# An attention and expert block: gate logits from the raw rows and centred weights, and two of four chunks routed inside the last attention round

## The reference, cut to what matters

```
x = x + attention(_layernorm(x))        # softmax(Q K^T / 4) V, then @ Wo + bo
h = _layernorm(x)
gate_logits = h @ gate_w.T              # 8 logits a row
top_vals, top_idx = top_k(gate_logits, 2)
w = softmax(top_vals)
x = x + sum over the two chosen e of w_e * (h @ expert_w[e].T + expert_b[e])
```

## Time and profile before

| | us |
|---|---|
| three runs | 1721.37, 1722.83, 1723.59 (median 1722.83) |
| profiled execution, its own time | 1721.14 |
| its span in the trace | 1719.2 |
| TensorE busy | 1634.2 (95%) |
| VectorE, ScalarE, POOL busy | 83%, 75%, 33% |
| share of the chain of waits that is TensorE | 87% |
| first product with Wo starts | 1447.31 |
| first slot's transposes start | 1537.85 |
| TensorE's last product ends | 1695.67 |
| mean granted clock of TensorE | 0.981 |

### The profile page before, as it was taken

The page is one execution under the profiler, slowest core; times in us unless marked ns, Lnnn a source line. Parts: engine busy times, 40 slices in busy tenths (PEclk is TensorE's granted clock), DMA queues, the critical chain, the costliest instruction groups (busy, mean ns, idle before and its releaser), DMA issues.

```text
span 1719.2 us, 38275 instructions
## 1 busy us (share of the span) xinstructions
PE 1634.2 (95%) x13793; PEld 797.7 (46%) x13794; DVE 1423.8 (83%) x1694; ACT 1286.5 (75%) x2417; POOL 564.4 (33%) x828
## 2 busy tenths in 40 slices
PE   6999999999999999999999999999999999876994
PEld 3533444444444444444444444444444445655883
DVE  4488999999999999999999999999999942645455
ACT  3226888888888888888888888888888897333552
POOL 3121243333333333333333333333333445333221
PEclk9999999999999999999999999999999999978997
DMA  6434345423343333233223323322322142754566
GB/s 202 114 104 118 74 100 113 85 67 91 76 90 71 91 76 76 67 91 86 69 67 91 73 81 84 98 67 67 91 68 35 42 138 71 290 190 134 154 210 252
DMA packets 86838, 179.03 MB, mean 104 GB/s; under 512 B 20206, under 2 KB 24318, under 8 KB 85936
## 3 DMA queue, kind: packets, MB, share of 16 engines
q1 hardware_dynamic: 50464, 87.22, 21.2%
q0 software_dynamic: 34656, 88.26, 16.4%
q10 hardware_dynamic: 1584, 1.57, 0.3%
HBM read 91.14 MB, written 86.23 MB: 103 GB/s over the span
## 4 chain that ended last, share of the span: by engine, by line
PE 87%; DMA 3%; POOL 2%; issue 2%; ACT 2%; DVE 1%; SPq 1%; another core or an unknown queue 1%; ACTq 0%; POOLq 0%; DVEq 0%
PE bank L1026 32%; PE bank L987 25%; PE bank L1016 14%; PE bank L1112 6%; PE bank L957 5%; PE bank L1158 1%; DMA x_all<-in_L_attn_x 1%; ACT o_acc L815 1%; PE bank L1204 1%; PE bank L978 1%; DMA scratch<-y_rows 1%; POOL x_all L531 1%; PE bank L1218 1%; DMA sums<-o_acc 0%
## 5 line engine op out<-in xcount | busy, mean ns | idle before, releaser
L1304 DVE TENSOR_REDUCE max_kc<-bank 128x1 f32<-128x1024 f32 x1024 | 1243.4, 1222 | 64.9 <-PE bank L987 48.9
L838 ACT ACTIVATE arena_p<-bank 128x512 f32<-128x512 f32 x2048 | 1109.7, 595 | 160.6 <-PE bank L1016 120.7
L1026 PE MATMUL bank<-arena_p,v_cur 128*32 128x256 f32 x8192 | 653.5, 391 | 10.6 <-ACT o_acc L815 10.6
L987 PE MATMUL bank<-k_st,q_st 48*128 48x512 f32 x2048 | 511.2, 496 | 0.8 <-ACT qf L785 0.8
L1016 PE MATMUL bank<-q_st,k_st 50*128 50x512 f32 x2048 | 441.6, 406 | 0.8 <-ACT arena_p L838 0.8
L987 PEld LDWEIGHTS bank<-k_st,q_st 48*128 48x128 f32 x2048 | 190.5, 183 | 428.3 <-issue 398.7
L1016 PEld LDWEIGHTS bank<-q_st,k_st 50*128 50x128 f32 x2048 | 295.1, 185 | 33.0 <-ACT arena_p L838 21.7
L1026 PEld LDWEIGHTS bank<-arena_p,v_cur 128*32 128x32 f32 x8192 | 162.4, 108 | 296.3 <-issue 152.3
L483 POOL DMA_DIRECT2D sums<-o_acc x128 | 64.8, 513 | 343.3 <-ACT o_acc L815 338.0
L957 PE MATMUL bank<-xT,arena_p 128*128 128x512 f32 x160 | 84.9, 644 | 5.7 <-DMA arena_p<-in_L_attn_bv 3.6
L486 POOL DMA_DIRECT2D sums_rec<-sums x32 | 18.2, 570 | 210.6 <-DVE sums L1334 210.6
(11 more groups left out here) (193 smaller groups left out, 1015.8 us busy)
## 6 DMA issues: line engine op xcount, KB each, us to landing
slots_x<-pad_row POOLq DMA_DIRECT2D x27, 1295.0 KB, 5.8
q_st<-q_parts SPq DMA_DIRECT2D x192, 128.0 KB, 4.4
xs<-slots_x SPq DMA_DIRECT2D x39, 259.0 KB
q_parts<-parts SPq DMA_DIRECT2D x16, 512.0 KB, 3.2
we_raw<-in_L_ffn_expert_w POOLq DMA_DIRECT2D x8, 1024.0 KB, 6.1
at_parts<-o_hl POOLq DMA_DIRECT2D x128, 64.0 KB, 2.3
we_his<-o_hl POOLq DMA_DIRECT2D x32, 256.0 KB, 2.4
we_hi<-we_his SPq DMA_DIRECT2D x8, 1024.0 KB
```

The source lines that it names most:

```text
L838: act.activation(probs[:, u % PRING, :], bank[:, ring_bank(("score", u)), :], ACT.Exp, scale=SCALE).then_inc(p_ready, 1)
L987: return pe.matmul(bank[:, 2 + 2 * (m % 2) + q, :], q_st[r:r + CROW, j % SLOTS, h, qt * P:(qt + 1) * P], k_st[r:r + CROW, key_slot(j // NC ...
L1026: mm = pe.matmul(bank[32 * h:32 * h + 32, 6, half], v_cur[:, kt, :], probs[:, (REP * kt + h) % PRING, half], start=(kt == 0 and part == 0) ...
L1304: dve.reduce_max(max_kc[:, m:m + 1], bank[:, 2 + 2 * (m % 2):4 + 2 * (m % 2), :].rearrange("p a s -> p (a s)"), AX.X).then_inc(m_done, 1)
```

## The change

**What it does.** With the second layer norm written out, a logit is (r·(W − mean W))·rstd, r being the raw row and mean W each expert's mean weight, so the row need not be normalised before the gates. The raw row is x + attention·Wo + bo. The x part comes from the first layer norm's rows, times their standard deviation: eight centred gate columns are put behind the 128 columns of Wv (`GV` = 136), with the mean taken off by `centre_gates`. The part of `bo` is four small products. Attention's part uses Wo·gates: Wo is transposed in round 30 (`turn_wo`), multiplied with the gates (`wo_gates`) and kept as `wowc`. A chunk's logits are then eight products of `wowc` with the chunk's attention outputs (`gate_logits`). Choices need no rstd; the difference of the two logits gets it inside the exponential.

Chunks 0 and 1 are routed in round 31 (table `GATES`: key tile, step), chunks 2 and 3 at tiles 8 and 12. Per tile, ScalarE keeps only the square root and TensorE only the three terms, in four banks. Scatters 0 to 3 are issued within and behind `divide_outputs(N)`, each tile's scatter waiting for its own statistics. `biases_split` moves from tile 9 to tile 6, `load_attention(1)` also waits for Wo·gates, `place_rows(3)` goes to slot 0, and the last additions for three chunks to slots 1, 2 and 3. At the start the loads get semaphores of their own, bv is no longer waited for before the projection, weights go over ScalarE's queue, and the loads of x's chunks 1 to 3 wait for Wk and Wq.

The diff, cut to its core:

```diff
-        GT_BANKS = [n % 2 for n in range(NKT - 2)] + [2, 3]
+        WO_BANKS, LG_BANK, RK_BANK, XT_BANK = (2, 3, 0, 1), 4, 5, 6
+        TURN_WO, WO_GATES = (11, 12), 14
+        LOGITS_AT, BACK_AT, RANKS_AT = {8: 2, 12: 3}, {8: 2, 12: 3}, {10: 2, 15: 3}
+        GATES = {3: ("logits", 0), 5: ("back", 0), 6: ("logits", 1), 8: ("ranks", 0), 10: ("back", 1), 13: ("ranks", 1)}
...
+            def scatter(n):
+                c = n // TT
+                if n == 0:
+                    pool.wait_ge(fill_dma, 16 * -(-NX // FILL))
+                    pool.wait_ge(tok_ready, NC - 1)
+                if n % TT == 0:
+                    pool.wait_ge(slots_ready, c + 1)
+                    if c == NC - 1:
+                        pool.wait_ge(tok_ready, NC)
+                pool.wait_ge(nmr_ready, n + 1)
+                for a in range(2):
+                    pool.indirect_dma_start(slots_x, bass.IndirectOffsetOnAxis(ap=slot_i[:, a, n:n + 1], axis=0),
+                                            x2_all[:, n, :], None).then_inc(sc_dma[c], 16)
...
                 pool.dma_start(sums_rec.rearrange("h (a q) -> (h a) q", a=32), sums[:, :]).then_inc(rec_dma, 16)
+                if i == N:
+                    scatter(0)
                 pool.wait_ge(rec_dma, 16 * i)
                 for h in range(REP):
                     pool.dma_start(rec_b[32 * h:32 * h + DK, :], sums_rec[h].partition_broadcast(DK)).then_inc(recb_dma, 16)
+                if i == N:
+                    scatter(1)
...
             divide_outputs(N)
+            for n in range(2, TT):
+                scatter(n)
             add_bias_o(NC - 1)
...
+            sp.wait_ge(wk_dma, 16)
+            sp.wait_ge(wq_dma, 16)
             for c in range(1, NC):
                 sp.dma_start(x_all[:, c * TT:(c + 1) * TT, :], x_t[:, c * TT:(c + 1) * TT, :]).then_inc(x_dma[c], 16)
+            for t in range(TT):
+                sp.dma_start(bv_sb[:, t, :], bv.partition_broadcast(P)).then_inc(bv_dma, 16)
...
                 if c == 1:
                     sp.wait_ge(v_ready, G)
+                    sp.wait_ge(ww_full, 1)
...
+            act.dma_start(wk_sb[:, :, :], Wk.rearrange("(k p) n -> p k n", p=P)).then_inc(wk_dma, 16)
+            act.wait_ge(consts, 6)
+            act.dma_start(wg_sb[:, :, 0:E], gate_w.rearrange("(k p) n -> p k n", p=P)).then_inc(wg_dma, 16)
+            act.dma_start(wq_sb[:, :, :], Wq.rearrange("(k p) n -> p k n", p=P)).then_inc(wq_dma, 16)
+            act.dma_start(bo_col[:, :], bo.rearrange("(k p) -> p k", p=P), allow_slow_non_contiguous=True).then_inc(bc_dma, 16)
+            act.dma_start(wv_sb[:, :, 0:KVD], Wv.rearrange("(k p) n -> p k n", p=P)).then_inc(wv_dma, 16)
...
-            act.wait_ge(fill_dma, 16 * -(-NX // FILL))
-            act.wait_ge(pv_done, PRING // REP + NKT * N)
-            for n in range(NKT + 2):
-                if n >= 3:
-                    gate_evac(n - 3)
-                if n >= 6 and n % TT == 2:
-                    logits_evac((n - 6) // TT)
-                if 1 <= n <= NKT:
-                    deviation2(n - 1)
-                    normalise_tile(n - 1)
+            for n in range(NKT):
+                deviation2(n)
+                if n in LOGITS_AT:
+                    logits_evac(LOGITS_AT[n])
...
+                    pe.wait_ge(wk_dma, 16)
+                if c == 0:
+                    pe.wait_ge(wg_dma, 16)
+                    pe.wait_ge(pool_step, 4)
+                    for k in range(KD):
+                        mm = pe.matmul(bank[:, 5, 304:304 + E], ones[:, :], wg_sb[:, k, 0:E], start=(k == 0),
+                                       stop=(k == KD - 1))
+                    mm.then_inc(gm_full, 1)
...
+            pe.wait_ge(gm_taken, 2)
+            pe.wait_ge(bc_dma, 16)
+            for k in range(KD):
+                mm = pe.matmul(bank[:, 5, 304:304 + E], bo_col[:, k:k + 1].to_broadcast([P, P]), wg_sb[:, k, 0:E],
+                               start=(k == 0), stop=(k == KD - 1))
+            mm.then_inc(bg_full, 1)
...
+            def turn_wo(j):
+                if j == 0:
+                    pe.wait_ge(wo_dma, 16)
+                    pe.wait_ge(m_done, 2 + MUNITS * N)
+                for k in range(KD):
+                    mm = pe.transpose(bank[:, 2 + j, k * P:(k + 1) * P], wo_raw[:, k, j * P:(j + 1) * P], ident[:, :])
+                mm.then_inc(woT_full, 1)
+            def wo_gates():
+                pe.wait_ge(woT_evac, KD)
+                for k in range(KD):
+                    for j in range(KD):
+                        mm = pe.matmul(bank[:, 2, k * 32:(k + 1) * 32], wo_t[:, j, k * P:(k + 1) * P], wg_sb[:, j, :],
+                                       start=(j == 0), stop=(j == KD - 1))
+                mm.then_inc(ww_full, 1)
+            def gate_logits(k):
+                if k == 0:
+                    pe.wait_ge(ww_ready, 1)
+                else:
+                    pe.wait_ge(lgT_ready, k)
+                pe.wait_ge(at_dma[k % 2], 32 * (k // 2 + 1))
+                for part in range(2):
+                    for d in range(KD):
+                        mm = pe.matmul(bank[32 * d:32 * d + 32, LG_BANK, :], wowc[:, d, :],
+                                       at_hl[k % 2][part][:, d, :].bitcast(F32), start=(part == 0), stop=(part == 1),
+                                       skip_group_check=True)
+                mm.then_inc(lg_full, 1)
...
+                if i == N - 2 and kt in TURN_WO:
+                    for j in range(2):
+                        turn_wo(2 * TURN_WO.index(kt) + j)
+                if i == N - 2 and kt == WO_GATES:
+                    wo_gates()
+                if i == N - 1 and kt in GATES:
+                    gates_step(*GATES[kt])
...
+            def attention_tile(n):
                 c, q = n // TT, slice(n % TT * P, (n % TT + 1) * P)
-                if term == 0:
-                    pe.wait_ge(at_dma[c % 2], 32 * (c // 2 + 1))
-                    pe.wait_ge(x2_ready, n + 1)
-                part, w = [(0, wo_hi), (1, wo_hi), (0, wo_lo)][term]
-                for k in range(KD):
-                    mm = pe.matmul(bank[:, WO_BANKS[n % 3], :], at_hl[c % 2][part][:, k, q], w[:, k, :],
-                                   start=(term == 0 and k == 0), stop=(term == 2 and k == KD - 1))
-                if term == 2:
-                    mm.then_inc(wo_full, 1)
...
-            pe.wait_ge(wc_dma, 16 * (2 + E))
+                pe.wait_ge(at_dma[c % 2], 32 * (c // 2 + 1))
+                if n >= len(WO_BANKS):
+                    pe.wait_ge(x2_ready, n - len(WO_BANKS) + 1)
+                product(bank[:, WO_BANKS[n % len(WO_BANKS)], :],
+                        [lambda k: at_hl[c % 2][0][:, k, q], lambda k: at_hl[c % 2][1][:, k, q]],
+                        [lambda k: wo_hi[:, k, :], lambda k: wo_lo[:, k, :]]).then_inc(wo_full, 1)
...
             for n in range(NKT):
-                attention_tile(n, 0)
-                if n >= 3:
-                    gate_logits(n - 3)
-                attention_tile(n, 1)
-                if n >= 6 and n % TT == 2:
-                    logits_back((n - 6) // TT)
-                attention_tile(n, 2)
-                if n >= 7 and n % TT == 3:
-                    ranks((n - 7) // TT)
-                if n >= 2:
-                    gate_transpose(n - 2)
-            gate_logits(NKT - 3)
-            gate_transpose(NKT - 2)
+                if n in LOGITS_AT:
+                    gate_logits(LOGITS_AT[n])
+                attention_tile(n)
+                if n in BACK_AT:
+                    logits_back(BACK_AT[n])
+                if n in RANKS_AT:
+                    ranks(RANKS_AT[n])
...
+            def centre_gates():
...
+                dve.wait_ge(gm_full, 1)
+                dve.wait_ge(wv_dma, 16)
+                sums_ = bank[:, 5, 304:304 + E].unsqueeze(1).to_broadcast([P, KD, E])
+                dve.scalar_tensor_tensor(wv_sb[:, :, KVD:GV], sums_, -1.0 / D, wg_sb[:, :, 0:E], ALU.mult,
+                                         ALU.add).then_inc(gm_taken, 1)
...
+            def evacuate_values(b):
+                tiles, both = slice(2 * b, 2 * b + 2), bank[:, 4 + b % 2, 0:2 * GV].rearrange("p (t n) -> p t n", t=2)
+                g0 = chosen[:, tiles, :]
+                dve.wait_ge(v_full, b + 1)
+                dve.tensor_tensor(v_all[:, tiles, :], both[:, :, 0:KVD], bv_sb[:, 0:2, :], ALU.add).then_inc(v_evac, 1)
+                dve.tensor_tensor(g0, both[:, :, KVD:GV], std2[:, tiles].unsqueeze(2).to_broadcast([P, 2, E]),
+                                  ALU.mult).then_inc(g0_evac, 1)
+                dve.wait_ge(g0_evac, b + 1)
+                dve.tensor_tensor(g0, g0, bo_gate[:, :].unsqueeze(1).to_broadcast([P, 2, E]), ALU.add).then_inc(g0_step, 1)
...
+            for j in range(KD):
+                turned_wo(j)
+            lower_wo()
+            take_gates()
+            logits_evac(0)
+            reciprocal_sums(N - 1)
+            choose_first(0)
```

(32 more changed lines are left out.)

352 lines of the change are left out of this document (159 added, 193 removed).

## The result

The changed kernel takes 1746.28 us (median of four runs, 1741.88 to 1749.87) against 1722.91 us for the kernel before (four runs, 1721.37 to 1723.59): the ratio is 1.0124, with a 95% interval of 1.0100 to 1.0148. The profiled execution took 1749.63 us, its span is 1747.9. Of the four executions two took 1741.88 and 1742.92 us at a mean granted clock of 0.973 and 0.974, and two 1749.63 and 1749.87 at 0.967 and 0.965: one slow stretch of 17 us fewer would make that difference of the clock (an estimate: 17 us at half clock are 0.005 of the span). The table is of the longer kind.

A forecast was written before the change was run, and what follows sets the result against it. TensorE was taken as the bound (95% busy, 87% of the chain of waits). Start -1.5, rounds +8, Wo stage +8 and slots -19 summed to -4.5 us on 1721.1, giving 1716.6 us, range 1700 to 1729.

The forecast's parts named there:

- The rounds: Rounds 30 and 31: 13.9 us of work inserted on TensorE, partly hidden, adds 8 us; bounds +4 and +13.9.
- each insertion is hidden for about 0.6 us: Rounds 30 and 31: ScalarE's queued score banks cover about 0.6 us of each of nine insertions, 5.4 us in all.
- the upper bound: Rounds 30 and 31: none of the inserted work is hidden, +13.9 us.
- rival 3: Rounds 30 and 31: insertions hidden as far as the queue allows, 1711 us, or (upper side, chance 0.10) not at all, 1722.5.
- The Wo stage: First Wo product to slots: DVE waits for memset and biases, delaying the serial chain; +8 us, bounds -12 and +20.
- rival 2: Wo stage: TensorE at the 1.2 GHz level through tiles 8 to 15, +11.5 us, total 1728 us; chance 0.16.
- the small load cannot pass the large ones: Wo stage: the bias load queues behind 9.44 MB of loads, landing about 46.3 us after the first Wo matmul.
- Rival 1: Wo stage: transfers don't hold DVE, so the chain ends 11 us earlier, total 1705.6 us; chance 0.24.
- The slots: The 39 slots: the gap before slot 9 goes, 138.6 us in all, -19 us; bounds -20 and -10.
- rival 4: Slots: slot 9 is still late by half of the gap, +9 us, total 1725.6 us; chance 0.08.
- The start: Kernel start: the projection no longer waits for bv, less added small matmuls, -1.5 us; bounds -3.0 and +3.
- the lower bound of -3.0: Kernel start: the most it could gain, the projection beginning at 14.82 us instead of 17.82.

The follow-up runs named there:

- e7_filler: e6 plus one unread 512-column product behind each turn-back and each ranks step in round 31; ratio 0.9984 to the kernel before.
- f2: Kernel before plus 1, 1 and 5 unread products of 512 columns at key tiles 11, 12 and 14 of round 30; ratio 1.0013.
- f3: Kernel before plus 16 unread 128-column transposes at key tiles 11 and 12 of round 30; ratio 0.9994.
- e1: Changed kernel with biases_split back behind tile 9; median 1736.92 us, ratio 1.0079 to the kernel before.
- e2: Changed kernel with the 16 products of Wo with the gates in four pieces at key tiles 13, 14, 15 and 0; ratio 1.0100 to the kernel before.
- e3: Changed kernel with attention chunk 2 issued before all weight loads, chunk 3 and the biases after two of them; median 1740.51 us, ratio 1.0109 to the kernel before.
- e6: e5 with the products of Wo with the gates in four pieces, as in e2; median 1713.93 us, ratio 0.9936 to the kernel before.
- after: The profiled execution of the changed kernel itself, with no further edit; 1749.63 us.
- e4: Changed kernel with scatters 2 and 3 behind the bias addition of chunk 3; median 1748.99 us, ratio 1.0147 to the kernel before.
- e5: Changed kernel with biases' memset, load and split later (split behind tile 15), ranks of chunk 2 behind tile 11, attention chunks issued as in e3; 1719.71 us, ratio 0.9970.
- r1: The changed kernel run again unaltered on another group's chip; median 1747.63 us, ratio 1.0144 to the kernel before.
- f1: Kernel before plus 16 unread 128-column transposes and 16 unread 32-column products in round 30; median 1747.99 us, ratio 1.0142.
- f5: Kernel before plus only the unread 32-column products at key tile 14 of round 30; ratio 1.0121.
- f4: f1 plus two unread 512-column products at key tile 15 of round 30 and two at key tile 1 of round 31; ratio 1.0039 to the kernel before.
- e8: e6 with the logits of chunk 1 behind the first ranks in round 31; ratio 0.9986 to the kernel before.
- r2: e6 run again beside r1 on one chip; median 1708.68 us, ratio 0.9924 to the kernel before.

## Why the prediction was wrong, step by step

**The rounds (+8 forecast, +27.8 measured) are the step that failed**, and twice. First, "each insertion is hidden for about 0.6 us" was wrong. Where the clock stayed up (e7_filler, less its 3.7 us of filler) the rounds took 69.5, 14.1 more than before: the whole of the 13.9 us of inserted work, which was the upper bound and the upper side of rival 3. f2 and f3 show the same in the kernel before, 6.5 us for 6.5 of work and 2.0 for 2.1. TensorE writes the scores just ahead of ScalarE, so ScalarE's wait (1.50 us behind 1.02 of transposes) was longer than the insertion. The trace of the kernel before had it already, in ScalarE's timeline of round 30, where ScalarE waits for scores between some key tiles, so that no scores lay in reserve:

```profile
1403.50 2.06 ACT L838 ACTIVATE arena_p<-bank 128x512 f32<-128x512 f32 x4 [0.18 <-PE bank L1016]
1405.74 2.06 ACT L838 ACTIVATE arena_p<-bank 128x512 f32<-128x512 f32 x4 [0.18 <-PE bank L1016]
```

Second, the sum had no term for the clock here. Traces with one slow stretch of 17 to 20 us have rounds of 75.3 to 77.7 (e1, e2, e3, e6), with two 81.9 to 84.8 (after, e4, e5, r1): 6 to 8 us for each. I read the falls of the clock in the earlier trace rows as the price of idling, and looked for them only where TensorE would wait. That reading was too simple for the kernel before, too, where not "each such wait" is followed by a slow stretch: the one of 2.19 us at 1471.73 is not. In round 30 the clock fell while TensorE was busy in every window. The experiments showed the trigger of that stretch (32-column products with the weight loads full, f1 and f5 against f2 and f3) and the cure (512-column products, f4). The trigger of the stretch in round 31 is not shown.

**The Wo stage (+8, +14.2)**: the mechanism was right, its size was off. Forecast and measured, in us after the first Wo product: VectorE idle until 31, then 29.5; the biases land at 46.3, then 49.1; the turn-back of logits 2 at about 54, then 55.2; tile 10 ends at 63.9, then 64.1; the ranks of chunk 2 at 68.7, then 70.3; the last product at 92, then 96.3; the slots at 98.5, then 104.8. So 1.0 of the 6.3 us too much had arisen by the turn-back and 4.3 by the last product; the last 2.0 lie behind it, where TensorE waits 4.23 us for VectorE before the ranks of chunk 3. What the 3.3 us in between are was not taken apart. Slow clock is the likely part of it, which would be rival 2 in part: its sign, 0.50 in most windows from 50 us on, held for 27 of 55 us, and between tile 7 and the slots the granted clock was at 0.50 for some 45 us (22 in the whole stage before), in part of which TensorE idled. That the small load cannot pass the large ones held: e3 moved it in the queue and it landed 9 us after the memset in place of nearly 20, e4 gave the memset 5 us and it landed no sooner. Rival 1, with transfers that do not hold VectorE, is thereby excluded (it is also the rival meant where the prediction says "the second rival's time"). Not foreseen was that attention chunk 2 itself came 9.09 us late for tile 8, behind two weight loads; VectorE's lag covered it.

**The slots (-19, -14.1)**: the gap before slot 9 is gone, as forecast, and rival 4 with it. The 39 slots cost 39 x 3.44 = 134.2, and 9.6 beside it where I had 4: the first takes 7.42, at slow clock, with a wait of 0.43 in it, and four more waits of 0.56 to 1.48 us on ScalarE and VectorE lie in the slots up to slot 8. No run was made to take these apart.

**The start (-1.5, -0.3)**: the sign was right; one trace of each says little. The first product for the maxima comes at 76.92, 80.42, 77.66, 79.35, 78.82 and 79.65 us in the six traces with the old start (mean 78.8), and at 73.2 to 76.8 in the twelve with the new one (mean 75.5); the gain is about 3 us, the lower bound of -3.0. The first projection began at 14.27, as forecast near 15.

**The sum**: in the traces, 14 us of work moved to where TensorE was full, 14 more of slow clock there, and 14 in the Wo stage, where VectorE waits for the memset and the biases, against 14 from the slots.

## What to carry to other kernels

Before work is put into a stretch where TensorE looks as if it had slack, see who sets the pace there and how far ahead TensorE is: with none, every microsecond counts in full. Here narrow products in pieces of 1.1 us, or with 512-column products behind them, cost little more than their own time in round 30; read the granted clock behind such products, since an engine at half clock is busy all the same. A wait for a small load took, here, the time of what was issued before it on the queue: moving the load helped by 9 us of the Wo stage (e3), moving memset, load and split to where they are needed by 28 (e5).

## What the runs showed of the hardware

- TensorE's granted clock fell to its 1.2 GHz level while TensorE was busy in each window, during or just behind 3.8 to 4.6 us of 32-column products with full weight loads (nine of nine traces), and not behind 128-column transposes of 1.0 us twice (f3), nor behind 4.6 us of 512-column products (f2), nor behind four pieces of 1.1 us (six of six traces).
- Once down, it stayed down for 61 us (f1, f5) under the rounds' own alternating score and value products, with TensorE busy but for 0.2 us, and came back in the value products at their end, about 1 us before the first Wo product. Where 512-column products followed (f4), it came back 3.4 us after the fall; adding 3.7 us of such products took 17.7 us off.
- The Trainium skill (TensorE: Matmul & The Clock Gate, "HAM oscillation — how this bites in real kernels") lays a clock that falls again within a kernel to TensorE's waits for data, and "Part 1: The HAM clock gate (the "warmup" mystery)" has sustained matmul activity bring it back. In f1 neither fits: it fell with TensorE busy for 2.00 of 2.00 us, and 61 us of products, with one pause of 0.2 us in the trace, went by before it rose. Here the measurement decides: the form of the products counts, too.
- The same kernel before took 1711.55 us on one chip and 1722 to 1724 on three others. On that chip its Wo stage took 75.0 and 74.9 us (f3, f4, with unread work in round 30), against 84 to 91 elsewhere (before, f1, f2, f5), while the Wo stage of e6 took 77.6 there (e7, e8) and 77.8 on two other chips (e6, r2). Why is open.
